# Two transformer layers with a mixture of experts on one core: routing of batch 0 inside the attention, shared experts of chunk 1 behind the expert blocks

## What is computed

```python
scores = softmax(xf @ gate_w.T)                 # 8 experts
topk_w, topk_i = top_k(scores, 2); topk_w /= sum(topk_w)
y = sum over e of cw[:, e] * ((silu(xf @ wg[e]) * (xf @ wu[e])) @ wd[e])
shared = (silu(xf @ sg) * (xf @ su)) @ sd       # inner size 256
x = layernorm(xf + y + shared)
```

## Time and profile before

| | us |
|---|---|
| median of 3 runs | 717.64 (717.23 to 723.69) |
| the profiled execution | 718.89 |
| its span | 717.1 |
| PE busy | 648.1 |
| VectorE busy | 412.5 |
| ScalarE busy | 394.5 |
| POOL busy | 233.0 |

### The profile page before, as it was taken

The page is one execution under the profiler, slowest core; times in us unless marked ns, Lnnn a source line. Parts: engine busy times, 40 slices in busy tenths (PEclk is TensorE's granted clock), DMA queues, the critical chain, the costliest instruction groups (busy, mean ns, idle before and its releaser), DMA issues. The chain is left out here.

```text
span 717.1 us, 11088 instructions
## 1 busy us (share of the span) xinstructions
PE 648.1 (90%) x3717; PEld 301.7 (42%) x3717; DVE 412.5 (58%) x1069; ACT 394.5 (55%) x565; POOL 233.0 (32%) x255
## 2 busy tenths in 40 slices
PE   4998899999998979999969999999999889999870
PEld 1654422222431344445422222243344657877450
DVE  1478616334466696979451333245738846547697
ACT  1235679988586832545438888867775133333100
POOL 0002533335412223113341344523122705325250
PEclk9998599999998989879898999999999999999996
DMA  8500143333224422310415545433570253575331
GB/s 276 168 0 16 43 74 54 58 57 57 39 37 68 67 71 70 67 53 1 67 32 86 83 79 84 81 64 62 90 225 1 97 190 126 175 235 164 102 119 59
DMA packets 52105, 62.68 MB, mean 87 GB/s; under 512 B 10150, under 2 KB 38819, under 8 KB 51891
## 3 DMA queue, kind: packets, MB, share of 16 engines
q1 hardware_dynamic: 48971, 53.50, 33.1%
q0 software_dynamic: 3072, 8.39, 3.8%
HBM read 28.79 MB, written 18.35 MB: 66 GB/s over the span
## 5 line engine op out<-in xcount | busy, mean ns | idle before, releaser
L1411 ACT ACTIVATE probs<-ps 128x1024 f32<-128x1024 f32 (+1 forms) x320 | 276.2, 963 | 67.6 <-PE ps L1329 67.5
L1329 PE MATMUL ps<-ops_mem 99*128 99x512 bf16 (+3 forms) x768 | 165.7, 338 | 10.8 <-issue 6.8
L1346 PE MATMUL ps<-probs,vstat 128*32 128x512 f32 (+3 forms) x1536 | 169.0, 512 | 7.1 <-DVE raw L1251 6.3
L1422 POOL TENSOR_SCALAR_AFFINE_SELECT probs<-probs 128x512 f32<-128x512 f32 x128 | 84.6, 661 | 210.6 <-ACT probs L1411 210.0
L1329 PEld LDWEIGHTS ps<-ops_mem 99*128 99x128 bf16 x768 | 58.3, 99 | 159.8 <-ACT probs L1411 86.3
L1251 DVE COPY raw<-ps 128x512 f32<-128x512 f32 x32 | 22.1, 691 | 141.9 <-PE ps L1346 141.7
L1346 PEld LDWEIGHTS ps<-probs,vstat 128*32 128x32 f32 x1536 | 31.3, 109 | 70.9 <-issue 47.6
L2278 PE MATMUL ps<-parts_mem 128*128 x184 | 47.4, 381 | 0.3 <-ACT parts_mem L2159 0.3
L2122 POOL DMA_INDIRECT yT<-made,w1qkv x32 | 30.5, 954 | 47.0 <-DMA made<-parts_mem 37.8
L2113 POOL DMA_INDIRECT sent<-xres,w1qkv x32 | 30.8, 964 | 39.8 <-DVE w1qkv L615 22.2
L1720 PE MATMUL ps<-ops_mem,w1qkv 128*128 128x512 f32 x64 | 36.4, 698 | 0.1
(11 more groups left out here) (214 smaller groups left out, 937.3 us busy)
## 6 DMA issues: line engine op xcount, KB each, us to landing
ops_mem<-parts_mem SPq DMA_DIRECT2D x276, 64.0 KB
sent<-in_zero_row SPq DMA_DIRECT2D x2, 2944.0 KB, 67.9
made<-parts_mem SPq DMA_DIRECT2D x46, 128.0 KB, 1.8
probs<-sent SPq DMA_DIRECT2D x4, 896.0 KB, 8.8
ops_mem<-parts_mem SPq DMA_DIRECT2D x66, 32.0 KB
yT<-in_xT SPq DMA_DIRECT2D x4, 512.0 KB, 7.6
xres<-in_x SPq DMA_DIRECT2D x1, 2048.0 KB, 14.5
parts_mem<-in_wgu SPq DMA_DIRECT2D x2, 1024.0 KB
```

The lines of the kernel that those rows point to most:

```text
L1329: last = nc.tensor.matmul(ps[:, bank, o:o + CH - lo], kT[0:KDIM, buf, h if kh == GH else 0, kt * P:(kt + 1) * P], qT[0:KDIM, buf, h, c * C ...
L1346: last = nc.tensor.matmul(ps[32 * h:32 * h + 32, AV, lo:CH], vstat[:, i % 2, kt, h if kh == GH else 0, :], probs[:, s % PRING, h, 0:CH - l ...
L1411: nc.scalar.activation(o, banks, ACT.Exp, scale=score_scale).then_inc(s_exp, 1)
L1422: nc.gpsimd.affine_select(out=block_, in_=block_, compare_op=ALU.is_ge, fill=0.0, base=0, pattern=[[0, GH], [1, P]], channel_multiplier=-1 ...
```

## The change

Routing of batch 0 moves forward. VectorE evicts both projections of chunk 1 ahead of item 5; it normalises chunk 0 between item 5's halves and chunk 1 behind them; the copies of chunk 0's transposes stand behind that and ahead of item 6; transposes and logits of chunk 1 are all in item 6; `choose` stands ahead of item 7, `rank` at its step 8 in bank 7, and `seat` between its halves. The small weights of the rank are loaded first, on a semaphore of their own. In `tail` PE does gate and up of chunk 0 first and then projects chunk 2; gate, up and down of chunk 1 go behind the blocks. `accumulate` of chunks 1 to 3 adds to what `weigh` has put there, `weigh` of these starts from the row itself, and `weigh(1)` moves into the blocks.

```diff
             def beside(self, pe, i, s):
-                for m, steps in enumerate((((4, 8), (4, 10)), ((5, 2), (5, 6)))):
+                for m, steps in enumerate((((4, 8), (4, 10)), ((5, 2), (5, 4)))):
                     if (i, s) in steps:
                         self.project(pe, m, steps.index((i, s)))
-                for m, steps in enumerate((((5, 11), (6, 2)), ((6, 11), (7, 2)))):
+                for m, steps in enumerate((((5, 10), (6, 2)), ((6, 6), (6, 8)))):
                     if (i, s) in steps:
                         self.turn(pe, m, steps.index((i, s)))
-                if (i, s) in ((6, 4), (7, 4)):
-                    m = i - 6
+                if (i, s) in ((6, 4), (6, 10)):
+                    m = int(s == 10)
                     pe.wait_ge(self.s_xT, 2 * (m + 1))
                     self.seven(pe, self.LOGIT[m])
                     self.logits(m, 7).then_inc(self.s_seven, 1)
+                if (i, s) == (7, 8):
+                    pe.wait_ge(self.s_chosen, 1)
+                    pe.wait_ge(s_rank_w, 48)
+                    self.seven(pe, self.RANKS)
+                    self.rank(pe, 0, 7).then_inc(self.s_seven, 1)
             def before(self, dve, i):
                 if i == 5:
                     self.sum(dve, 1, 0)
+                    self.sum(dve, 1, 1)
                 if i == 6:
-                    self.of.k.then(self.of.statistics(0, y_sums[1]))
-                if i >= 6:
-                    self.evicted(dve, self.LOGIT[i - 6])
-                    self.keep_logits(i - 6, 7).then_inc(self.s_evicted, 1)
+                    self.keep_turned(dve, 0, 1)
+                    self.keep_seven(dve, 0)
+                if i == 7:
+                    self.choose(dve, 0)
             def between(self, dve, i):
...
                 if i == 5:
-                    self.sum(dve, 1, 1)
-                if i in (5, 6):
                     self.of.scale()
-                    self.of.apply(x_of(i - 5)).then_inc(self.s_norm, 1)
-                    self.keep_turned(dve, i - 5, 0)
+                    self.of.apply(x_of(0)).then_inc(self.s_norm, 1)
+                    self.norm(dve, 1)
+                    self.of.k.then(self.of.statistics(0, y_sums[1]))
+                if i == 6:
+                    self.keep_turned(dve, 1, 0)
+                    self.keep_turned(dve, 1, 1)
+                    self.keep_seven(dve, 1)
+                    self.shift(dve, 0)
                 if i == 7:
-                    self.shift(dve, 0)
-                    self.choose(dve, 0)
+                    self.evicted(dve, self.RANKS)
+                    self.keep_rank(7).then_inc(self.s_evicted, 1)
+                    dve.wait_ge(self.s_evicted, self.RANKS + 1)
+                    self.seat(dve, 0)
             def behind(self, dve, i):
...
                 if i == 5:
-                    self.norm(dve, 1)
-                if i in (5, 6):
-                    self.keep_turned(dve, i - 5, 1)
+                    self.of.scale()
+                    self.of.apply(x_of(1)).then_inc(self.s_norm, 1)
+                    self.keep_turned(dve, 0, 0)
...
-                        if route and (i, s) == (NI - 1, 8):
+                        if route and (i, s) == (NI - 1, 1):
                             route.exp(act, 0)
...
-                bank_free(pe)
-                project(2)
                 pe.wait_ge(s_exp_w, 16 * len(expert_weights))
-                route.rank(pe, 0)
                 gate_up(0)
                 gate_up(1)
+                bank_free(pe)
+                route.seven(pe, route.RANKS + 1)
+                project(2)
                 project(3)
...
-                gate_up(2)
-                gate_up(3)
-                down(1)
...
+                gate_up(2)
+                gate_up(3)
                 gate_up(4)
+                down(1)
                 gate_up(5)
...
-                    if n == 38:
+                    if n == 36:
                         weigh(0, (0, 1))
+                    if n == 37:
+                        weigh(0, (2, 3))
                     if n == 39:
-                        weigh(0, (2, 3))
-                    if n == 41:
                         of = normalised(0, range(CT))
                         statistics(of)
+                    if n == 41:
+                        scaled(of, 0)
                     if n == 43:
-                        scaled(of, 0)
+                        weigh(1, (0, 1))
+                    if n == 44:
+                        weigh(1, (2, 3))
+                multiplied(2)
+                multiplied(3)
                 multiplied(4)
-                weigh(1, range(CT))
+                accumulate(1)
                 multiplied(5)
...
                 multiplied(6)
+                weigh(2)
                 accumulate(2)
-                weigh(2, range(CT))
                 multiplied(7)
...
+                weigh(3)
                 for n, (lo, hi) in enumerate(LAST):
...
-                    weigh(3, range(lo, hi))
```

More of the change, by code:

```diff
@@ L2153, in _ @@
                 route.exp(act, 1)
-                silu(2)
-                silu(3)
                 def keep_block(n):
@@ L2261, in turn_block @@
                     if n == 0:
-                        pe.wait_ge(s_dve_tail, dve_at["mul", 2])
+                        pe.wait_ge(s_dve_tail, dve_at["sum", 0])
                     for kk in range(2):
```

93 lines of the change are left out of this document (45 added, 48 removed).

## The result

The changed kernel takes 735.86 us (median of 4 runs, 733.28 to 736.75), the kernel before 720.66 beside it: 1.0222 times as long, 95% interval 1.0179 to 1.0266. In two more sets of runs it took 739.36 (ratio 1.0255, 1.0190 to 1.0319) and 738.46 (1.0244, 1.0194 to 1.0293). The forecast was 729.5 with a range up to 734: the direction and the places were right, the size was 6 to 10 us short, and the time lies outside the range. The forecast added 11.9 to a kernel before at 717.64; beside the kernel before of its own set the changed kernel took 15.2, 20.2 and 16.4 more.

What follows compares the result with a forecast made beforehand. TensorE was taken to bound attention and blocks, VectorE the stretch behind them. First `hidden` 1.6 later, blocks 1.0 and end 9.3 sum to 11.9 us, taking the median 717.64 to 729.5; range 722.5 to 734.

Steps and rivals of the forecast that it cites:

- The wait at (6, 2): Item 6, second transpose of chunk 0: TensorE waits 6.4 us for VectorE's copy, low bound 6.1, high 7.0.
- Rival A: Item 6: VectorE reaches the copy before TensorE needs it, so no wait; 7.1 us goes away, 722.4; chance 0.08.
- The clock behind it: Item 6, after TensorE's idle time: the clock may stay at its lower level for a while; 0.7 us, between 0 and 1.7.
- The wait in item 7: Item 7's first output waits for VectorE's normalise and choice of experts: 1.4 us, up to 2.3, taken as 1.7.
- The front: From TensorE's last values product in the attention to VectorE's first `hidden`: 35.7 us, with 5.0 for the down product.
- Blocks: In the block loop VectorE gets `weigh(1)` more, beyond its slack between blocks: 1.0 us added, between 0 and 3.
- End part: From the end of the blocks to VectorE's end: its unbroken work starts late, 52.1 us against 42.8, so +9.3.
- Rival B: Low clock comes often: 1.0 us more at item 6, another 1.7 in item 7's wait; about 732; chance 0.15.

## Why the prediction fell short

- *The wait at (6, 2)*: 6.4 worked out, 6.40 or 6.41 measured in the four traces that keep VectorE's order and leave TensorE idle. Right. Rival A is out.
- *The clock behind it*: taken as 0.7 "between 0 and 1.7". This step failed. I priced the low clock by one stretch seen elsewhere and reasoned that item 6's own stretch "may only be moved". It was lengthened: it cost about 4.5 us more than before in two traces and 1.5 in the third, and it was gone where TensorE was given work in the wait. The rule of the Trainium skill that I weighed ("TensorE: Matmul & The Clock Gate", section "What's actually happening") would have brought the sum 1.0 nearer and not far enough. The traces agree with it that the clock falls to half where TensorE has no work (0.50 from about 506, in the wait from 503.4 on).
- *The wait in item 7*: 1.7 for the wait and VectorE's stretched operations, with nothing for the clock. The gap is 1.33; with its slow products it is 2.7 (20.8 against 18.1) in all three traces of the changed kernel, and 1.1 where no low clock came (19.2, in two traces of other kernels with the same wait). Low by 1.0, and by the same step: the clock behind a wait.
- *The front*: 35.7 from the last values product, measured 39.5. The second failed step, and the same one: I took 5.0 for the down but full speed for the transposes and logits. The logits alone are 1.6 over, the down 0.9, the transposes 0.4; the remaining 0.9 is the sum and norm of chunk 2 on VectorE (7.2 where I took 6.7) and small differences. With TensorE kept busy it was 35.1.
- *Blocks*: +1.0, measured +1.7 to +2.2. *End part*: +9.3, measured +8.4 to +9.1. Near enough. But the reason given for the second, that only VectorE's start counts, held for this order alone (the kernel with the down early).
- *Rival B*, the clock comes often, had 0.15 and 732. It is what happened, and its 732 was still 4 to 7 too low. Over the table's five stretches the forecast gives +11.9 and the traces +20.9, +22.0 and +18.3. Items 6 and 7 and the front together are 9.4, 9.3 and 6.4 of what is missing, most of it low clock.

The medians differ by less than the traces (15.2 in the first set, against 20.9): the first trace reached item 5 3.1 earlier than that of the kernel before, and the start of the second layer lies anywhere from 383 to 391 in the traces, at 386.5 to 391.4 where the granted clock of the first 380 us is 0.91, and at 383.1 to 386.7 where it is 0.93 or 0.94.

## To carry to other kernels

Where TensorE is the bound, a wait of it can cost more than its gap: price it once by the gap alone and once with the work behind it at half the clock, since both happened here (item 7: 1.1 and 2.7 for the same gap), and add this up over all waits, also the short ones. Before moving work behind a stage, look where TensorE waits within it and put the work there; the same instructions in another order differed by 8.4 us between the medians, 5.8 of it in the front of the traces. A copy that frees a bank goes ahead of work that no one is waiting for yet.

## What the runs showed of the hardware

- After 6.41 us without work on TensorE the granted clock stayed at 0.50 for up to 13 us of work that looked dense in the timeline. The same work behind 5 us of repeated transposes and a wait of 1.02 ran at the full clock throughout (one trace).
- Low stretches also came behind short waits: in the front each trace of the changed kernel, with waits of 2.22 and 1.16, had 0.50 for about 10 us, from the transposes to near the end of the down (about 578 to 588 in the first). With the waits filled it was gone, up to the wait of 1.01 ahead of the first block, where one came again. But a short wait does not always bring one: behind the 1.33 us in item 7 it came in five traces of seven. And one came without a wait, behind the logits of item 6, in the kernel before and in six of nine traces of the new order.
- The extent of a low stretch behind the same wait varied between traces (item 6 of 36.5, 36.4, 33.5 and 33.4). A single trace prices it badly.
- 44 transposes of 128x128 in a row took 5.03 us, 0.114 each; a group of four shows 0.66 in the timeline, so that a long row can't be priced from it.
